# Another order for the five engines' queues in a graph-attention and expert-attention kernel

## The chip, the cores and the metric

The kernel runs on one core of one Trainium2 chip. The metric is device time in microseconds of one execution, taken as the median of several. The profile is that of one execution on the same core.

## The reference

Two layers on `x` of shape 128 graphs x 128 tokens x 384 channels, `adj` of 128 x 128 x 128:

```python
# layer A: graph attention, 12 heads of 32
h = layernorm(x)
q, k = h @ Wq.T, h @ Wk.T;  v = h @ Wv.T + bv
scores = einsum('bqhd,bkhd->bhqk', q, k) * 384**-0.5 + 2 * adj
p = softmax(scores)                  # rows without any score that is not 0 are left out
x = x + einsum('bhqk,bkhd->bqhd', p, v).reshape(b, n, 384) @ Wo.T + bo
# layer B: three causal attention experts of 128 channels, gated
h = layernorm(x)
gate = softmax(relu(h @ Wg1 + bg1) @ Wg2 + bg2)   # the two largest, renormalised: w_e
for e in range(3):
    qe, ke = parts of h @ Wqk + bqk; ve = h @ Wv[e] + bv[e]
    if e == 0: qe = depthwise_conv3(qe)           # e == 1: 4 more keys, all of them masked
    y[e] = softmax(causal(qe @ ke.T / sqrt(128))) @ ve
x = x + (y * w_e).reshape(...) @ Wp + bp
```

## The kernel before, in words

The 128 graphs are worked in 32 groups of 4 (`GB`). The work on a group is cut into steps. A step is named stage.kind.part (`A` for the first layer, `B` for the second, `W` for the weights' preparation at the start), and each engine has its own list of the steps in which it has a share. TensorE (PE) makes the product, ScalarE (ACT) and VectorE (DVE) take it out of its PSUM bank, GpSimd (POOL) scales, and SyncE (SP) issues transfers. The kinds:

- `hT`: four transposes of the normalised input. ACT writes the high f16 part, DVE the low part (what is left), and both feed later products. `qk.0` to `qk.5`: the projections to q and k, nine matmuls each (three passes over split operands). For A, ACT writes the high half and DVE the low one. `v.b`: the value projection of graph b.
- `A.score.b.c`: four heads of graph b (c = 0, 1, 2). DVE adds the adjacency and takes the row minimum into the single buffer `raw_score`, ACT exponentiates into `S[b % 2]`. `smax.b` is one DVE reduction over all of `raw_score`, and `norm.b` makes row factors on DVE and has POOL scale `S` with them. `B.score.b` is the same for three experts. `turn`: transposes of the scaled scores, copied out by ACT. `mix`: scores times values. `proj`: output projection, with the residual added by DVE. `ln1`, `ln2`: layernorm statistics on DVE, the rest on POOL. `res`: POOL adds a bias row to a whole group (1,536 columns). `B.gate.0/1/2` and `B.conv`: chains of small DVE instructions.
- `A.stack.0` and `A.stack.1` (SP): 12 transfers each, which restack q and k of the next group into `Qs` and `Ks`. `A.score.0.0` of that group waits for both of them. `stack.0` waits for the low half of `qk.2` and for the last score product of the group before, `stack.1` for the low half of `qk.5`. `A.adj` and `A.res` load the next adjacencies and inputs, `B.proj` stores.

Products of A go round 5 PSUM banks (`A_RING`), those of B round 3. A product waits until the step that stands 5 (3) places earlier among those of its stage in PE's list has been taken out (`wait_bank`). Bank, place and wait counts all follow from the lists, so the lists alone set the order of work.

A turn of the steady list `ORDER_OF_STEPS` works on three groups at once: the `hT`, `qk` and `stack` of A run one group ahead (`ahead`), the rest of A is on the group of the turn, and B is one group behind A. `FIRST_STEPS` is a list for the weights and the first two turns. Turns 2 to 33 take the steady list; in turn 32 what would be group 32 is left out, and turn 33 has B of group 31 alone. (Below, turn t begins with the product `A.score.0.0` of group t - 1.)

Of the kernel before, what the change touches and what calls it, by code (L numbers as in the profile page):

```python
# [46 lines left out]
NG = NB // GB  # L47
# [41 lines left out]
        W.turn.0@0 W.spread.0@0  # L89
        A.hT.0@0 A.hT.1@0 A.hT.2@0 A.qk.0@0 A.qk.1@0 A.qk.2@0 A.qk.3@0 W.turn.1@0 A.qk.4@0 W.spread.1@0  # L90
        A.qk.5@0 A.v.0@0 A.v.1@0 A.v.2@0 A.v.3@0 A.hT.0@1 A.hT.1@1 A.hT.2@1
        W.turn.2@0 W.spread.2@0 A.qk.0@1
        A.score.0.0@0 A.score.0.1@0 A.score.0.2@0 A.qk.1@1 A.score.1.0@0 A.qk.2@1
        A.score.1.1@0 A.score.1.2@0 A.qk.3@1 A.turn.0.0@0 A.turn.0.1@0 A.turn.0.2@0 A.score.2.0@0 A.mix.0@0
        A.score.2.1@0 A.score.2.2@0 A.qk.4@1 A.proj.0@0 A.turn.1.0@0 A.turn.1.1@0 A.turn.1.2@0
        A.score.3.0@0 A.mix.1@0 A.score.3.1@0 A.score.3.2@0 A.qk.5@1 A.proj.1@0 A.turn.2.0@0
        A.turn.2.1@0 A.turn.2.2@0 A.mix.2@0 A.proj.2@0 A.turn.3.0@0 A.turn.3.1@0 A.turn.3.2@0 A.mix.3@0 A.proj.3@0
    """,
    "act": """
        W.hi.0@0 A.hT.0@0 A.hT.1@0 A.hT.2@0 W.hi.1@0 A.qk.0@0 A.qk.1@0 A.qk.2@0 A.qk.3@0 A.qk.4@0  # L100
        W.hi.2@0 A.qk.5@0 W.stack.1@0 A.hT.0@1 A.hT.1@1 A.hT.2@1 W.hi.3@0 W.hi.4@0 A.qk.0@1 A.score.0.0@0 A.score.0.1@0
        A.qk.1@1 A.score.0.2@0 A.score.1.0@0 A.qk.2@1 A.score.1.1@0 A.score.1.2@0 A.qk.3@1
        A.turn.0.0@0 A.turn.0.1@0 A.turn.0.2@0 A.score.2.0@0 A.mix.0@0 A.score.2.1@0 A.score.2.2@0 A.qk.4@1
        A.turn.1.0@0 A.turn.1.1@0 A.turn.1.2@0 A.score.3.0@0 A.mix.1@0 A.score.3.1@0 A.score.3.2@0 A.qk.5@1
        W.hi.5@0 W.hi.6@0 A.turn.2.0@0 A.turn.2.1@0 A.turn.2.2@0 A.mix.2@0 A.turn.3.0@0 A.turn.3.1@0
        A.turn.3.2@0 A.mix.3@0 W.hi.7@0
    """,
    "dve": """
        W.max.0@0 W.max.1@0 W.share.0@0 W.scale.0@0 W.max.2@0 W.lo.0@0 A.hT.0@0 A.hT.1@0 A.hT.2@0
        W.lo.1@0 W.unit.0@0 A.qk.0@0 W.max.4@0 A.qk.1@0 W.max.5@0 A.qk.2@0 W.max.7@0 A.qk.3@0  # L110
        W.scale.1@0 A.qk.4@0 W.lo.2@0 A.qk.5@0 W.unit.1@0 W.values.0@0 A.v.0@0 A.v.1@0 A.ln1@0 A.v.2@0 W.max.3@0
        A.v.3@0 W.max.6@0 A.hT.0@1 A.hT.1@1 A.hT.2@1 W.scale.2@0 W.bias.0@0 W.unit.2@0 W.lo.3@0 W.lo.4@0 A.qk.0@1 A.score.0.0@0 A.score.0.1@0
        A.score.0.2@0 A.smax.0@0 A.qk.1@1 A.score.1.0@0 A.norm.0@0 A.qk.2@1 A.score.1.1@0 A.score.1.2@0
        A.smax.1@0 A.qk.3@1 A.norm.1@0 A.score.2.0@0 A.mix.0@0 A.score.2.1@0 A.score.2.2@0 A.smax.2@0
        A.qk.4@1 A.proj.0@0 A.norm.2@0 A.score.3.0@0 A.mix.1@0 A.score.3.1@0 A.score.3.2@0 A.smax.3@0
        A.qk.5@1 W.lo.5@0 A.proj.1@0 A.norm.3@0 W.lo.6@0 A.ln2.0@0 A.ln2.1@0 A.mix.2@0 A.proj.2@0
        A.ln2.2@0 A.mix.3@0 A.proj.3@0 A.ln2.3@0 W.lo.7@0
# [958 lines left out]
```

## Time and profile before

| | |
|---|---|
| median of 3 runs (lowest, highest) | 2308.9 us (2306.32, 2308.97) |
| the profiled execution's own time | 2308.58 us |
| its span from first to last instruction | 2306.8 us |
| PE, DVE, ACT, POOL busy | 2224.1, 1926.3, 1496.3, 1094.7 us |
| granted TensorE clock over the span | 0.99 |

The span is what the trace covers; the time is 1.8 us longer. A busy time is the union of an engine's instructions. An instruction that waits for a port or a semaphore inside its own execution counts as busy, so a duration that is above the usual one for its form is a wait too. In the timeline each row has the start in us from the span's start, the duration in us, the engine, the line, the operation with its tiles, how many instructions were merged, and in brackets how long the engine stood idle before it and what ended that.

### The profile page before, as it was taken

To read this page: it belongs to the slowest core of one execution; us is meant where nothing else is said; L and a number is where in the kernel's file an instruction comes from. 1 tells how busy PE (TensorE), PEld (TensorE's weight loads), DVE (VectorE), ACT (ScalarE), POOL (GpSimd) and SP (SyncE) were. 2 spreads that over 40 slices of the span, in tenths; PEclk is the share of its full clock that TensorE was granted. 3 is DMA by queue.
4 is the path that set the end of the run, shared out by engine and by line. 5 is a ranking of instruction groups with operands and counts; after the bars stand their busy time and mean duration, and the time that the engine had idled before them with its cause. 6 is when DMAs were issued, how large, how long until landed. Compare 5 with 4: busy or idle time off the path is not lost.

```text
span 2306.8 us, 51218 instructions
## 1 busy us (share of the span) xinstructions
PE 2224.1 (96%) x16905; PEld 1435.7 (62%) x16905; DVE 1926.3 (84%) x7160; ACT 1496.3 (65%) x5290; POOL 1094.7 (47%) x1351
## 2 busy tenths in 40 slices
PE   6799999999999999999999999999999999999998
PEld 3466666666666666666666666666666666666665
DVE  7788888888888888888888888888888888888884
ACT  2676666676666676666676666676666766666763
POOL 2454455444454544554544554544554544554442
PEclk9899999999999999999999999999999999999999
DMA  5221122221222221222221222211222211222100
GB/s 171 47 64 46 53 74 74 74 47 42 60 74 74 63 53 43 65 74 74 57 53 41 72 74 74 52 51 47 74 75 74 50 46 53 74 74 74 47 15 28
DMA packets 142263, 143.18 MB, mean 62 GB/s; under 512 B 16816, under 2 KB 141360, under 8 KB 142000
## 3 DMA queue, kind: packets, MB, share of 16 engines
q1 hardware_dynamic: 139808, 138.62, 22.6%
q8 instruction: 137, 2.24, 0.4%
q10 hardware_dynamic: 2192, 1.29, 0.2%
q14 instruction: 126, 1.03, 0.1%
HBM read 39.18 MB, written 25.17 MB: 28 GB/s over the span
## 4 chain that ended last, share of the span: by engine, by line
PE 81%; DVE 13%; issue 4%; ACT 1%; POOL 0%; DMA 0%; DVEq 0%; ACTq 0%; POOLq 0%
PE A_bank L465 29%; PE B_bank L465 28%; PE A_bank L536 7%; PE A_bank L548 4%; PE B_bank L555 4%; PE A_bank L523 4%; DVE raw_score L876 2%; PE B_bank L530 2%; PE B_bank L540 2%; PE B_bank L502 2%; DVE g_tmp L810 1%; DVE V L865 1%; DVE q2raw L798 1%; DVE x L916 1%; DVE g_tmp L801 1%
## 5 line engine op out<-in xcount | busy, mean ns | idle before, releaser
L1003 POOL TENSOR_TENSOR S<-S,rowf 128x512 f32<-128x512 f32 x384 | 389.0, 1041 | 663.2 <-DVE rowf L901 663.2
L638 ACT ACTIVATE S<-raw_score,smin 128x128 f32<-128x128 f32 x1536 | 593.7, 392 | 140.5 <-DVE smin L876 140.4
L876 DVE CUSTOM_DVE_ANT_0 raw_score<-A_bank,adj,s_unit 128x128 f32<-128x128 f32 x1536 | 442.5, 346 | 29.9 <-PE A_bank L523 29.7
L638 ACT ACTIVATION_READ_ACCUMULATOR S<-raw_score,smin 128x1 f32 x1536 | 294.7, 192 | 0.0
L652 ACT ACTIVATE PT<-A_bank 128x512 f32<-128x512 f32 x384 | 216.5, 592 | 106.7 <-PE A_bank L536 106.7
L1008 POOL TENSOR_TENSOR S<-S,row2f 128x384 f32<-128x384 f32 x128 | 105.9, 827 | 323.8 <-DVE row2f L909 321.2
L536 PE MATMUL A_bank<-ident,S 128*128 128x128 f32 x1536 | 218.7, 276 | 31.8 <-DVE x L916 29.6
L882 DVE TENSOR_REDUCE smax<-raw_score 128x12 f32<-128x1536 f32 x128 | 224.4, 1753 | 4.4
L536 PEld LDWEIGHTS A_bank<-ident,S 128*128 128x128 f32 x1536 | 181.3, 142 | 58.0 <-DVE x L916 35.3
L645 ACT ACTIVATE S<-S,s2min 128x128 f32<-128x128 f32 x384 | 148.8, 391 | 39.8 <-DVE s2min L886 39.8
L656 ACT ACTIVATE yT_hi<-B_bank 128x384 f16<-128x384 f32 x128 | 62.1, 485 | 164.1 <-PE B_bank L555 164.1
L523 PE MATMUL A_bank<-Ks,Qs 96*128 96x128 f16 x1536 | 134.4, 220 | 3.5 <-DVE k_lo L854 1.6
L465 PE MATMUL B_bank<-wv2g_hi,b_hT_hi 128*128 128x416 f16 x384 | 130.4, 339 | 0.0
L465 PE MATMUL B_bank<-wv2g_hi,b_hT_lo 128*128 128x416 f16 x384 | 130.1, 339 | 0.0
L465 PE MATMUL B_bank<-wv2g_lo,b_hT_hi 128*128 128x416 f16 x384 | 130.1, 339 | 0.0
L465 PE MATMUL A_bank<-wo_hi,oT_hi 128*128 128x384 f16 x384 | 125.9, 328 | 3.8 <-DVE oT_lo L859 3.8
L523 PEld LDWEIGHTS A_bank<-Ks,Qs 96*128 96x128 f16 x1536 | 108.2, 98 | 32.6 <-issue 7.3
L921 DVE SCALAR_TENSOR_TENSOR x1res<-B_bank,p_unit,x1res 128x384 f32<-128x384 f32 x128 | 78.8, 615 | 59.4 <-PE B_bank L465 59.4
L465 PE MATMUL A_bank<-wv_hi,a_hT_hi 128*128 128x384 f16 x384 | 125.4, 327 | 1.9 <-issue 1.5
L876 DVE DVE_READ_ACCUMULATOR2_ANT smin<- 128x1 f32 x1536 | 126.3, 82 | 0.0
L465 PE MATMUL A_bank<-wo_lo,oT_hi 128*128 128x384 f16 x384 | 126.0, 328 | 0.0
L465 PE MATMUL A_bank<-wo_hi,oT_lo 128*128 128x384 f16 x384 | 125.9, 328 | 0.0
(182 smaller groups left out, 6201.0 us busy)
## 6 DMA issues: line engine op xcount, KB each, us to landing
xin<-in_x SPq DMA_DIRECT2D x32, 768.0 KB, 4.7
Qs<-q_hi SPq DMA_DIRECT2D x256, 96.0 KB, 2.2
out<-x1res SPq DMA_DIRECT2D x128, 192.0 KB, 1.9
Ks<-k_hi SPq DMA_DIRECT2D x252, 96.0 KB, 2.6
Qs<-q_lo SPq DMA_DIRECT2D x128, 96.0 KB, 2.2
Ks<-k_lo SPq DMA_DIRECT2D x126, 96.0 KB, 2.2
adj<-in_adj SPq DMA_DIRECT2D x32, 256.0 KB, 3.5
S<-in_wq SPq DMA_DIRECT2D x1, 576.0 KB, 5.6
```

The lines of the kernel that those rows point to most:

```text
L465: mm = nc.tensor.matmul(dst, left(c)[a], right(c)[b], start=(c == 0 and n == 0), stop=(c == KC - 1 and n == 2))
L523: mm = nc.tensor.matmul(dst[:, tok(j)], Qs[:, c * HPC + j, tok(b)], Ks[:, c * HPC + j, tok(b)], start=True, stop=True)
L536: mm = nc.tensor.transpose(dst[:, tok(j)], S[b % 2][:, c * HPC + j, :], ident[:])
L548: mm = nc.tensor.matmul(dst[j * HD:(j + 1) * HD, tok(k)], V[:, b, h * HD:(h + 1) * HD], PT[k][:, tok(j)], start=True, stop=True)
L555: mm = nc.tensor.matmul(dst[:, tok(e)], V2[:, b, e * P:(e + 1) * P], PT2[b % 2][:, tok(e)], start=True, stop=True)
L638: ins = nc.scalar.activation(S[b % 2][:, h, :], raw_score[:, h, :], ACT.Exp, bias=smin[b % 2][:, h:h + 1], scale=-1.0, accum_out=ssum[b % ...
L645: ins = nc.scalar.activation(S2[b % 2][:, e, :], S2[b % 2][:, e, :], ACT.Exp, bias=s2min[b % 2][:, e:e + 1], scale=-1.0, accum_out=s2sum[b ...
L652: nc.scalar.activation(dst, src[:, 0:dst.shape[1]], ACT.Copy).then_inc(evacuated[stage, "act"], 1)
L876: ins = nc.vector.tensor_tensor_reduce(raw_score[:, h, :], src[:, j * T:(j + 1) * T], adj2[:, b, :], s_unit[:], 3.0e38, ALU.add, ALU.min, ...
L882: nc.vector.tensor_reduce(smax[b % 2][:], raw_score[:], AXX, ALU.max).then_inc(maxed, 1)
L1003: nc.gpsimd.tensor_tensor(S[b % 2][:, hs, :], S[b % 2][:, hs, :], rowf[b % 2][:, hs].unsqueeze(2).broadcast_to([P, HPC, T]), ALU.mult).the ...
L1008: nc.gpsimd.tensor_tensor(S2[b % 2][:], S2[b % 2][:], row2f[b % 2][:].unsqueeze(2).broadcast_to([P, NE, T]), ALU.mult).then_inc(normed2, 1)
```

## The change

No step's own instructions change, and every list has the same steps for the same groups as before. Changed are:

- the order in `FIRST_STEPS` (weights and the first two turns): among others `A.hT@1` and `A.qk@1` of PE move from before the first scores to between them, and `W.turn.2`, `W.spread.2` from behind `A.hT@1` to ahead of `A.v.0@0`
- the order in `ORDER_OF_STEPS` for PE, ACT, DVE and POOL (SP's is the same)
- turns 32 and 33, which no longer take the steady list but a new one, `LAST_STEPS`, in which the steps of groups 30 and 31 stand mixed (`@1` is group 30, `@0` is group 31)
- two waits on DVE that the new order needs (`w_lo`), both in the first two groups only

```diff
--- before.py
+++ after.py
@@ -86,79 +86,123 @@
 
 FIRST_STEPS = {
     "pe": """
...
+        W.turn.0@0 W.spread.0@0 A.hT.0@0 A.hT.1@0 A.hT.2@0 A.qk.0@0 A.qk.1@0 A.qk.2@0 A.qk.3@0 W.turn.1@0
+        W.spread.1@0 A.qk.4@0 A.qk.5@0 W.turn.2@0 W.spread.2@0 A.v.0@0 A.v.1@0 A.score.0.0@0 A.score.0.1@0
+        A.score.0.2@0 A.v.2@0 A.score.1.0@0 A.score.1.1@0 A.v.3@0 A.hT.0@1 A.hT.1@1 A.score.1.2@0 A.turn.0.0@0
+        A.turn.0.1@0 A.hT.2@1 A.score.2.0@0 A.score.2.1@0 A.qk.0@1 A.turn.0.2@0 A.qk.1@1 A.mix.0@0 A.score.2.2@0
+        A.turn.1.0@0 A.turn.1.1@0 A.qk.2@1 A.score.3.0@0 A.turn.1.2@0 A.score.3.1@0 A.qk.3@1 A.score.3.2@0
+        A.qk.4@1 A.mix.1@0 A.proj.0@0 A.turn.2.0@0 A.qk.5@1 A.turn.2.1@0 A.turn.2.2@0 A.proj.1@0 A.mix.2@0
+        A.turn.3.0@0 A.turn.3.1@0 A.turn.3.2@0 A.mix.3@0 A.proj.2@0 A.proj.3@0
     """,
     "act": """
...
     """,
     "dve": """
...
+        W.max.0@0 W.max.1@0 W.share.0@0 W.scale.0@0 W.unit.0@0 A.hT.0@0 W.lo.0@0 W.max.2@0 A.hT.1@0 A.hT.2@0
+        W.max.4@0 W.lo.1@0 A.qk.0@0 A.qk.1@0 W.max.7@0 A.qk.2@0 W.max.5@0 A.qk.3@0 W.max.3@0 W.scale.1@0
+        A.qk.4@0 W.max.6@0 A.qk.5@0 W.unit.1@0 W.lo.2@0 W.values.0@0 A.ln1@0 W.scale.2@0 A.v.0@0 A.v.1@0
+        A.score.0.0@0 A.score.0.1@0 A.v.2@0 A.score.0.2@0 A.smax.0@0 A.hT.0@1 A.score.1.0@0 A.norm.0@0 A.v.3@0
+        A.score.1.1@0 A.score.1.2@0 A.hT.1@1 A.smax.1@0 A.hT.2@1 A.score.2.0@0 W.unit.2@0 A.norm.1@0
+        A.score.2.1@0 A.qk.0@1 W.lo.3@0 A.qk.1@1 A.score.2.2@0 A.mix.0@0 A.smax.2@0 A.qk.2@1 A.score.3.0@0
+        A.score.3.1@0 A.score.3.2@0 A.qk.3@1 A.norm.2@0 W.lo.4@0 A.qk.4@1 A.proj.0@0 A.smax.3@0 A.mix.1@0
+        A.norm.3@0 A.qk.5@1 W.lo.5@0 A.proj.1@0 W.lo.6@0 A.ln2.0@0 A.mix.2@0 W.lo.7@0 A.ln2.1@0 A.proj.2@0
+        A.mix.3@0 A.ln2.2@0 W.bias.0@0 A.proj.3@0 A.ln2.3@0
     """,
     "pool": """
-        A.res@0 A.ln1@0 A.norm.0@0 A.norm.1@0 A.norm.2@0 A.ln2.0@0 A.norm.3@0 A.adj@0 A.ln2.1@0 A.ln2.2@0 A.ln2.3@0
+        A.res@0 A.ln1@0 A.norm.0@0 A.norm.1@0 A.norm.2@0 A.norm.3@0 A.adj@0 A.ln2.0@0 A.ln2.1@0 A.ln2.2@0
+        A.ln2.3@0
     """,
     "sp": """
-        A.res@0 A.stack.0@0 A.stack.1@0 A.adj@0 A.stack.0@1 A.stack.1@1
+        A.res@0 A.stack.0@0 A.stack.1@0 A.stack.0@1 A.adj@0 A.stack.1@1
     """,
 }
 
 ORDER_OF_STEPS = {
     "pe": """
-        A.score.0.0 A.v.0 A.score.0.1 A.v.1 A.score.0.2 A.v.2 A.v.3 B.hT.0 B.hT.1 A.score.1.0 B.hT.2
-        A.score.1.1 A.score.1.2 B.qk.0 B.qk.1 B.qk.2 B.v.0 A.turn.0.0 A.turn.0.1 B.qk.3 B.v.1
-        A.turn.0.2 A.score.2.0 B.v.2 A.mix.0 A.score.2.1 A.score.2.2 B.v.3 B.qk.4 B.qk.5 A.proj.0
-        B.score.0 A.hT.0 A.hT.1 A.turn.1.0 A.hT.2 B.score.1 A.turn.1.1 A.qk.0 A.turn.1.2 A.score.3.0
-        A.score.3.1 A.qk.1 A.qk.2 A.score.3.2 B.turn.0 A.qk.3 A.mix.1 A.qk.4 B.score.2 A.qk.5
-        A.turn.2.0 A.turn.2.1 B.turn.1 A.turn.2.2 A.proj.1 B.score.3 A.mix.2 B.mix.0 A.turn.3.0
-        A.turn.3.1 B.mix.1 A.turn.3.2 A.proj.2 B.turn.2 A.mix.3 B.proj.0 A.proj.3 B.mix.2 B.turn.3
-        B.proj.1 B.mix.3 B.proj.2 B.proj.3
+        A.score.0.0 A.score.0.1 A.v.0 A.v.1 A.score.0.2 B.hT.0 B.hT.1 B.hT.2 A.score.1.0 A.score.1.1 A.v.2
+        B.qk.0 B.v.0 B.v.1 A.score.1.2 B.qk.1 B.v.2 A.turn.0.0 A.v.3 A.turn.0.1 B.v.3 B.qk.2 A.turn.0.2 B.qk.3
+        A.hT.0 A.score.2.0 A.hT.1 A.mix.0 A.score.2.1 B.qk.4 A.hT.2 B.qk.5 A.turn.1.0 A.proj.0 B.score.0
+        A.turn.1.1 B.score.1 A.score.2.2 A.qk.0 A.turn.1.2 A.score.3.0 A.qk.1 A.qk.2 A.qk.3 B.turn.0 A.qk.4
+        B.mix.0 A.score.3.1 A.mix.1 A.score.3.2 B.turn.1 B.score.2 A.turn.2.0 A.qk.5 A.turn.2.1 A.proj.1
+        A.turn.2.2 B.score.3 B.mix.1 B.proj.0 A.mix.2 B.turn.2 B.proj.1 A.turn.3.0 B.mix.2 A.turn.3.1 A.turn.3.2
+        A.proj.2 B.turn.3 A.mix.3 B.mix.3 B.proj.2 A.proj.3 B.proj.3
     """,
     "act": """
...
+        A.score.0.0 B.hT.0 B.hT.1 B.hT.2 A.score.0.1 A.score.0.2 B.qk.0 A.turn.0.0 B.qk.1 A.score.1.0 A.turn.0.1
+        A.score.1.1 A.turn.0.2 B.qk.2 A.hT.0 A.score.1.2 A.hT.1 B.gate.0 A.mix.0 B.qk.3 A.hT.2 B.qk.4 B.qk.5
+        A.turn.1.0 A.score.2.0 A.turn.1.1 A.score.2.1 A.qk.0 B.gate.1 B.score.0 A.qk.1 A.turn.1.2 A.score.2.2
+        B.score.1 A.qk.2 B.turn.0 A.qk.3 A.qk.4 A.score.3.0 B.mix.0 A.mix.1 B.turn.1 A.turn.2.0 A.score.3.1
+        B.score.2 A.score.3.2 A.turn.2.1 A.turn.2.2 B.mix.1 A.qk.5 A.mix.2 B.turn.2 B.score.3 A.turn.3.0 B.mix.2
+        A.turn.3.1 A.turn.3.2 B.turn.3 A.mix.3 B.mix.3
     """,
     "dve": """
-        A.score.0.0 A.score.0.1 A.v.0 A.score.0.2 A.smax.0 A.v.1 B.hT.0 B.hT.1 B.hT.2 A.score.1.0
-        A.norm.0 A.ln1 A.v.2 A.v.3 A.score.1.1 B.conv B.v.0 A.score.1.2 A.smax.1 A.score.2.0 B.v.1 B.v.2
-        A.score.2.1 B.v.3 A.mix.0 B.gate.0 A.norm.1 B.gate.1 A.score.2.2 A.smax.2 A.proj.0 A.hT.0 A.hT.1
-        A.hT.2 B.score.0 B.gate.2 B.norm.0 B.score.1 A.qk.0 A.score.3.0 A.score.3.1 B.norm.1 A.qk.1
-        A.qk.2 A.norm.2 A.score.3.2 A.smax.3 A.ln2.0 A.mix.1 A.qk.3 B.score.2 A.qk.4 A.qk.5 A.norm.3
-        B.norm.2 B.score.3 A.proj.1 B.mix.0 A.mix.2 A.ln2.1 B.norm.3 A.proj.2 A.mix.3 A.ln2.2 B.mix.1
-        B.proj.0 A.proj.3 A.ln2.3 B.mix.2 B.proj.1 B.mix.3 B.proj.2 B.proj.3
+        A.score.0.0 A.v.0 A.score.0.1 A.score.0.2 B.hT.0 B.hT.1 B.hT.2 A.smax.0 A.v.1 A.score.1.0 B.v.0 A.norm.0
+        A.score.1.1 A.ln1 A.v.2 B.v.1 A.score.1.2 B.v.2 A.v.3 B.conv B.v.3 A.smax.1 B.gate.0 A.hT.0 A.norm.1
+        A.hT.1 A.score.2.0 A.mix.0 A.hT.2 A.score.2.1 B.gate.1 B.score.0 A.proj.0 A.score.2.2 B.score.1 B.gate.2
+        A.qk.0 B.norm.0 A.smax.2 A.qk.1 A.score.3.0 B.norm.1 A.norm.2 A.qk.2 A.qk.3 A.qk.4 A.score.3.1 A.mix.1
+        B.score.2 A.score.3.2 B.mix.0 A.smax.3 B.norm.2 A.norm.3 B.score.3 B.mix.1 A.qk.5 A.proj.1 B.proj.0
+        A.mix.2 B.norm.3 A.ln2.0 B.proj.1 A.ln2.1 B.mix.2 A.proj.2 A.mix.3 A.ln2.2 B.mix.3 B.proj.2 A.proj.3
+        A.ln2.3 B.proj.3
     """,
     "pool": """
-        A.res A.norm.0 A.ln1 B.res A.norm.1 B.norm.0 B.norm.1 A.norm.2 A.ln2.0 A.norm.3 A.adj
-        B.norm.2 A.ln2.1 B.norm.3 A.ln2.2 A.ln2.3
+        A.res A.norm.0 A.ln1 B.res A.norm.1 B.norm.0 B.norm.1 A.norm.2 B.norm.2 A.norm.3 B.norm.3 A.ln2.0
+        A.ln2.1 A.adj A.ln2.2 A.ln2.3
     """,
     "sp": """
         A.res A.stack.0 A.adj A.stack.1 B.proj.0 B.proj.1 B.proj.2 B.proj.3
+    """,
+}
+
+LAST_STEPS = {
+    "pe": """
+        A.score.0.0@0 A.score.0.1@0 A.v.0@0 A.score.0.2@0 B.hT.0@1 A.v.1@0 B.hT.1@1 A.score.1.0@0 B.hT.2@1
+        B.qk.0@1 B.v.0@1 A.score.1.1@0 A.score.1.2@0 B.v.1@1 B.v.2@1 B.qk.1@1 B.v.3@1 A.turn.0.0@0 A.score.2.0@0
+        B.qk.2@1 B.qk.3@1 B.qk.4@1 A.turn.0.1@0 A.score.2.1@0 A.turn.0.2@0 B.qk.5@1 A.score.2.2@0 B.score.0@1
+        A.mix.0@0 A.turn.1.0@0 A.turn.1.1@0 B.score.1@1 A.turn.1.2@0 A.score.3.0@0 A.v.2@0 A.score.3.1@0
+        B.turn.0@1 A.score.3.2@0 B.score.2@1 A.mix.1@0 A.proj.0@0 A.turn.2.0@0 A.turn.2.1@0 B.mix.0@1 B.turn.1@1
+        A.proj.1@0 A.turn.2.2@0 A.v.3@0 A.mix.2@0 A.turn.3.0@0 A.turn.3.1@0 A.turn.3.2@0 B.mix.1@1 B.proj.0@1
+        A.mix.3@0 A.proj.2@0 A.proj.3@0 B.score.3@1 B.turn.2@1 B.proj.1@1 B.mix.2@1 B.hT.0@0 B.hT.1@0 B.proj.2@1
+        B.hT.2@0 B.turn.3@1 B.qk.0@0 B.qk.1@0 B.mix.3@1 B.v.0@0 B.v.1@0 B.v.2@0 B.v.3@0 B.qk.2@0 B.qk.3@0
+        B.qk.4@0 B.qk.5@0 B.score.0@0 B.score.1@0 B.proj.3@1 B.turn.0@0 B.score.2@0 B.turn.1@0 B.mix.0@0
+        B.score.3@0 B.mix.1@0 B.proj.0@0 B.turn.2@0 B.mix.2@0 B.turn.3@0 B.proj.1@0 B.mix.3@0 B.proj.2@0
+        B.proj.3@0
+    """,
+    "act": """
...
+    """,
+    "dve": """
...
+    """,
+    "pool": """
+        A.norm.0@0 A.norm.1@0 B.res@1 A.res@0 B.norm.0@1 A.norm.2@0 B.norm.1@1 A.norm.3@0 A.ln2.0@0 A.ln2.1@0
+        B.norm.2@1 A.ln2.2@0 A.ln2.3@0 B.norm.3@1 A.adj@0 B.norm.0@0 B.norm.1@0 B.res@0 B.norm.2@0 B.norm.3@0
+        A.ln1@0
+    """,
+    "sp": """
+        A.adj@0 B.proj.0@1 A.res@0 B.proj.1@1 B.proj.2@1 B.proj.3@1 B.proj.0@0 B.proj.1@0 B.proj.2@0 B.proj.3@0
     """,
 }
 
@@ -180,12 +224,13 @@
     first = [parse(word) for word in FIRST_STEPS.get(engine, "").split()]
     order = [parse(word) for word in ORDER_OF_STEPS[engine].split()]
     program = list(first)
-    for turn in range(2 if first else 0, NG + 2):
+    last = [parse(word) for word in LAST_STEPS.get(engine, "").split()]
+    for turn in range(2 if first else 0, NG if last else NG + 2):
         for step in order:
             group = turn - (0 if ahead(step) else 1 if step[0] == "A" else 2)
             if 0 <= group < NG:
                 program.append((step, group))
-    return program
+    return program + [(step, NG - 1 - back) for step, back in last]
 
 
 GATE_LINKS = 17
@@ -861,6 +906,8 @@
                                             ALU.subtract).then_inc(freed, 1)
                 elif kind == "v":
                     wait_products(dve, step, g)
+                    if g == 0 and not A:
+                        dve.wait_ge(w_lo, len(raw))
                     V_b, row, col = (V[:, b, :], bv_row, 0) if A else (V2[:, b, :], bvg_row, 1)
                     nc.vector.scalar_tensor_tensor(out=V_b, in0=src[:, 0:row.shape[1]], scalar=v_unit[:, col:col + 1],
                                                    in1=row[:], op0=ALU.mult, op1=ALU.add).then_inc(freed, 1)
@@ -911,7 +958,9 @@
                     wait_products(dve, step, g)
 
                     dve.wait_ge(xres_ready, count(g, 1, 1))
-                    if not g == 0:
+                    if g == 0:
+                        dve.wait_ge(w_lo, 5)
+                    else:
                         dve.wait_ge(x1res_ready, count(g, 1, 0))
                     nc.vector.scalar_tensor_tensor(out=x1[:, b, :], in0=src[:, 0:C], scalar=p_unit[:, 0:1],
                                                    in1=xres[:, b, :], op0=ALU.mult, op1=ALU.add).then_inc(freed, 1)
```

## Rows read from the trace of the kernel before

**Rows 1.** The page: span, engine totals, the chain that ended last.

```profile
span 2306.8 us, 51218 instructions
PE 2224.1 (96%) x16905; PEld 1435.7 (62%) x16905; DVE 1926.3 (84%) x7160; ACT 1496.3 (65%) x5290; POOL 1094.7 (47%) x1351
PE 81%; DVE 13%; issue 4%; ACT 1%; POOL 0%; DMA 0%; DVEq 0%; ACTq 0%; POOLq 0%
```

**Rows 2.** Windows by stage: start:end, length, busy time of each engine, clock, DMA.

```profile
core 0: us, PE busy (x) PEld busy (x) DVE busy (x) ACT busy (x) POOL busy (x), PEclk, DMA share, GB/s
...
53.30:105.90 52.60, 36.16 (x275) 21.70 (x274) 35.64 (x138) 33.58 (x121) 17.84 (x25) 0.80 0.22 51
...
664.50:734.20 69.70, 68.68 (x531) 44.45 (x529) 59.19 (x222) 46.35 (x165) 34.20 (x43) 1.00 0.23 62
...
2198.00:2262.50 64.50, 59.91 (x464) 40.72 (x462) 54.98 (x205) 42.01 (x156) 26.96 (x34) 0.92 0.04 14
2262.50:2306.80 44.30, 35.76 (x200) 22.84 (x198) 19.75 (x70) 15.43 (x44) 6.74 (x5) 0.92 0.08 28
...
105.90:2198.00 2092.10, 2060.78 (x15841) 1333.70 (x15840) 1777.44 (x6663) 1390.93 (x4950) 1030.59 (x1265) 1.00 0.23 61
```

**Rows 3.** Timeline of turn 10 on PE: `B.score.1`, `turn.1.1`, `qk.0`; `B.score.2`.

```profile
697.95 0.83 PE L530 MATMUL B_bank<-k,q 128*128 128x128 f32 x6
699.77 0.66 PE L536 MATMUL A_bank<-ident,S 128*128 128x128 f32 x4 [0.99 <-DVE x L916]
700.46 0.38 PE L465 MATMUL A_bank<-a_hT_hi,wq_hi 128*128 128x512 f16 x1
...
712.51 0.83 PE L530 MATMUL B_bank<-k,q 128*128 128x128 f32 x6
713.18 0.38 PE L465 MATMUL A_bank<-a_hT_hi,wk_hi 128*128 128x512 f16 x1
```

**Rows 4.** The same turn, DVE: `smax.2` and `A.proj.0`; all waits for A products.

```profile
697.43 1.75 DVE L882 TENSOR_REDUCE smax<-raw_score 128x12 f32<-128x1536 f32 x1
699.10 0.61 DVE L916 SCALAR_TENSOR_TENSOR x<-A_bank,p_unit,xres 128x384 f32<-128x384 f32 x1
...
PE A_bank L536 <- DVE x L916: 29.6, 30, 1.0
```

**Rows 5.** K restack in turn 10: `qk.5` low half, SP's issues; landing medians.

```profile
715.95 0.69 DVE L854 SCALAR_TENSOR_TENSOR k_lo<-A_bank,k_hi 128x512 f16<-128x512 f32 x1 [0.60 <-ACT k_hi L613]
...
717.68 3.78 SPq L440 DMA_DIRECT2D Ks<-k_hi  x4
...
724.08 2.56 SPq L440 DMA_DIRECT2D Ks<-k_hi  x4
...
Ks<-k_hi SPq DMA_DIRECT2D x8, 96.0 KB, 2.4
```

**Rows 6.** DVE instructions with two SBUF operands, against POOL (turns 10 and 32).

```profile
694.42 0.82 DVE L810 TENSOR_TENSOR g_tmp<-g_tmp,g_col 128x12 f32<-128x12 f32 x1
694.17 3.05 POOL L1003 TENSOR_TENSOR S<-S,rowf 128x512 f32<-128x512 f32 x3 [6.91 <-DVE rowf L901]
...
2213.08 3.81 DVE L938 SCALAR_TENSOR_TENSOR q<-q2raw,conv_neg,q 128x508 f32<-128x508 f32 x1
2212.46 3.89 POOL L997 TENSOR_TENSOR x1res<-x,bp_row 128x1536 f32<-128x1536 f32 x1
```

**Rows 7.** Opening: PE ahead of `hT@1`, DVE and POOL steps, the last K issues.

```profile
32.48 0.68 DVE L854 SCALAR_TENSOR_TENSOR k_lo<-A_bank,k_hi 128x512 f16<-128x512 f32 x1
...
53.27 1.15 PE L523 MATMUL A_bank<-Ks,Qs 96*128 96x128 f16 x11
...
97.34 3.04 POOL L1003 TENSOR_TENSOR S<-S,rowf 128x512 f32<-128x512 f32 x3
...
89.56 0.69 DVE L854 SCALAR_TENSOR_TENSOR k_lo<-A_bank,k_hi 128x512 f16<-128x512 f32 x1 [0.86 <-ACT k_hi L613]
...
101.17 2.54 SPq L440 DMA_DIRECT2D Ks<-k_hi  x4
```

More of the change, by code:

```diff
@@ L88 @@
     "pe": """
[L89 to L95, printed above, removed]
@@ L96 @@
-        A.score.3.0@0 A.mix.1@0 A.score.3.1@0 A.score.3.2@0 A.qk.5@1 A.proj.1@0 A.turn.2.0@0
-        A.turn.2.1@0 A.turn.2.2@0 A.mix.2@0 A.proj.2@0 A.turn.3.0@0 A.turn.3.1@0 A.turn.3.2@0 A.mix.3@0 A.proj.3@0
+        W.turn.0@0 W.spread.0@0 A.hT.0@0 A.hT.1@0 A.hT.2@0 A.qk.0@0 A.qk.1@0 A.qk.2@0 A.qk.3@0 W.turn.1@0
+        W.spread.1@0 A.qk.4@0 A.qk.5@0 W.turn.2@0 W.spread.2@0 A.v.0@0 A.v.1@0 A.score.0.0@0 A.score.0.1@0
+        A.score.0.2@0 A.v.2@0 A.score.1.0@0 A.score.1.1@0 A.v.3@0 A.hT.0@1 A.hT.1@1 A.score.1.2@0 A.turn.0.0@0
@@ L98 @@
+        A.turn.0.1@0 A.hT.2@1 A.score.2.0@0 A.score.2.1@0 A.qk.0@1 A.turn.0.2@0 A.qk.1@1 A.mix.0@0 A.score.2.2@0
+        A.turn.1.0@0 A.turn.1.1@0 A.qk.2@1 A.score.3.0@0 A.turn.1.2@0 A.score.3.1@0 A.qk.3@1 A.score.3.2@0
+        A.qk.4@1 A.mix.1@0 A.proj.0@0 A.turn.2.0@0 A.qk.5@1 A.turn.2.1@0 A.turn.2.2@0 A.proj.1@0 A.mix.2@0
+        A.turn.3.0@0 A.turn.3.1@0 A.turn.3.2@0 A.mix.3@0 A.proj.2@0 A.proj.3@0
     """,
     "act": """
-        W.hi.0@0 A.hT.0@0 A.hT.1@0 A.hT.2@0 W.hi.1@0 A.qk.0@0 A.qk.1@0 A.qk.2@0 A.qk.3@0 A.qk.4@0
@@ L101 @@
[L101 to L105, printed above, removed]
@@ L106 @@
-        A.turn.3.2@0 A.mix.3@0 W.hi.7@0
+        A.hT.0@0 W.hi.0@0 W.hi.1@0 A.hT.1@0 A.hT.2@0 A.qk.0@0 A.qk.1@0 A.qk.2@0 A.qk.3@0 A.qk.4@0 A.qk.5@0
+        W.hi.2@0 W.stack.1@0 W.hi.3@0 W.hi.4@0 A.score.0.0@0 A.score.0.1@0 A.hT.0@1 A.score.0.2@0 A.hT.1@1
+        A.score.1.0@0 A.score.1.1@0 A.turn.0.0@0 A.hT.2@1 A.turn.0.1@0 W.hi.5@0 A.score.1.2@0 A.qk.0@1
+        A.turn.0.2@0 A.score.2.0@0 A.qk.1@1 A.mix.0@0 W.hi.6@0 A.turn.1.0@0 A.turn.1.1@0 A.score.2.1@0 A.qk.2@1
+        A.score.2.2@0 A.turn.1.2@0 A.qk.3@1 A.score.3.0@0 W.hi.7@0 A.qk.4@1 A.score.3.1@0 A.mix.1@0
@@ L107 @@
+        A.score.3.2@0 A.turn.2.0@0 A.qk.5@1 A.turn.2.1@0 A.turn.2.2@0 A.turn.3.0@0 A.mix.2@0 A.turn.3.1@0
+        A.turn.3.2@0 A.mix.3@0
     """,
     "dve": """
[L109 to L117, printed above, removed]
+        W.max.0@0 W.max.1@0 W.share.0@0 W.scale.0@0 W.unit.0@0 A.hT.0@0 W.lo.0@0 W.max.2@0 A.hT.1@0 A.hT.2@0
@@ L137 @@
+        A.turn.1.1 B.score.1 A.score.2.2 A.qk.0 A.turn.1.2 A.score.3.0 A.qk.1 A.qk.2 A.qk.3 B.turn.0 A.qk.4
+        B.mix.0 A.score.3.1 A.mix.1 A.score.3.2 B.turn.1 B.score.2 A.turn.2.0 A.qk.5 A.turn.2.1 A.proj.1
+        A.turn.2.2 B.score.3 B.mix.1 B.proj.0 A.mix.2 B.turn.2 B.proj.1 A.turn.3.0 B.mix.2 A.turn.3.1 A.turn.3.2
+        A.proj.2 B.turn.3 A.mix.3 B.mix.3 B.proj.2 A.proj.3 B.proj.3
     """,
     "act": """
-        A.score.0.0 A.score.0.1 B.hT.0 B.hT.1 B.hT.2 A.score.0.2 B.qk.0 A.score.1.0 B.qk.1 B.qk.2
@@ L140 @@
-        A.turn.0.0 A.turn.0.1 B.qk.3 A.score.1.1 A.turn.0.2 A.score.1.2 A.mix.0 A.score.2.0
-        A.score.2.1 B.gate.0 B.qk.4 B.qk.5 A.hT.0 A.hT.1 A.turn.1.0 B.gate.1 A.hT.2 A.turn.1.1
-        B.score.0 A.qk.0 A.score.2.2 A.turn.1.2 B.score.1 A.qk.1 A.qk.2 A.score.3.0 A.score.3.1
-        A.mix.1 A.qk.3 A.qk.4 B.turn.0 A.score.3.2 A.qk.5 B.score.2 A.turn.2.0 B.turn.1 A.turn.2.1
-        A.turn.2.2 A.mix.2 B.mix.0 A.turn.3.0 A.turn.3.1 A.turn.3.2 B.score.3 B.mix.1 B.turn.2
-        A.mix.3 B.mix.2 B.turn.3 B.mix.3
+        A.score.0.0 B.hT.0 B.hT.1 B.hT.2 A.score.0.1 A.score.0.2 B.qk.0 A.turn.0.0 B.qk.1 A.score.1.0 A.turn.0.1
```

19 lines of the change are left out of this document (added).

## The prediction, made before the changed kernel was run

> **What bounds the kernel now.** I read the page first. PE is busy for 96% of the span and holds 81% of the chain that ended last; DVE has 84% and 13% [rows 1]. A busy share is a mean over stages, so I next cut the span where `A.score.0.0` of a group starts [rows 2]. Thirty steady turns take 105.9 to 2198.0, 2092.1 us, so 69.74 us each. What lies around them is 105.9 us ahead and 108.8 us behind (64.5 and 44.3). In a steady turn the clock is full and PE is busy for 68.68 of 69.70 us; ACT with 46 us and POOL with 34 us have much room, DVE with 59 us has some. In turn 1 PE is busy for 36.2 of 52.6 us at a mean clock of 0.80, in the last window for 35.8 of 44.3 us. So a new order can win little per turn, but thirty times, and it can win more per microsecond at the two ends.
>
> The timeline of PE in a steady turn shows where the idle microsecond lies. `B.score.1` starts at 697.95, and the next product, `A.turn.1.1`, starts 1.82 us later; after `B.score.2` the same distance is 0.67 us [rows 3]. That is a stall of 1.15 us. The four transposes of `turn.1.1` then take 0.69 us up to `qk.0`; four in a row elsewhere take 0.44 us, which is 0.25 us more. What ends the wait is DVE's `A.proj.0`: five places back in A's ring of banks stands `proj.0`, and DVE takes it out at 699.10 only, since `smax.2` (1.75 us) stands ahead of it in DVE's list [rows 4]. The view of waits has this 30 times, 29.6 us, once a turn [rows 4]. It costs 1.15 + 0.25 = 1.40 us a turn.
>
> **The change, part by part.** *The steady turn.* Nothing is added or removed, so PE's work in a turn stays, and the best turn is 69.74 - 1.40 = 68.34 us. (Small delays of about 0.05 to 0.1 us at four other places, together 0.26 us, may go or stay. I leave them in the sum; 68.1 us is the low bound.) In the new list the product five places ahead of `turn.1.1` is `mix.0`, not `proj.0`. To see when DVE is done with it I laid the new lists side by side, gave each step the duration that it has in turn 10, started PE at 0 with no stall, and let each step of ACT, DVE and POOL begin when its list and its input allow. DVE takes `mix.0` out at 29.4 us, and PE wants the bank at 32.9: 3.5 us to spare. The same walk gives the other tight places: `A.proj.0` needs `mix.0` 1.3 us before its turn; `A.turn.1.0` needs the bank of `score.2.0` with 1.4 us to spare; `A.turn.3.0` waits for the low half of `qk.5` with 2 us to spare; `B.mix.3` gets its transposes from ACT with 0.2 us to spare, which is thin, but a miss there costs tenths. `B.hT.0` wants all of `ln2` from POOL 1.6 us after it is ready. No place costs a whole microsecond, and I find no new stall.
>
> *What gets later: the K restack.* Before, DVE takes `qk.5` at 715.95 and is done at about 716.6. SP issues 12 transfers from 717.68 to 726.64 and the last lands 2.4 us later, near 729.0 [rows 5], 5.2 us before the next turn. In the new lists `qk.5` starts on PE 48.2 us after the turn's start (48.7 before), but on ACT and DVE it stands behind `B.mix.1`, whose product ends 4 us later still. The walk has its low half done at 56.0 us. From SP's first Ks issue to the last landing is 11.4 us by the rows, so Ks is there at 67.5 us, and the next `A.score.0.0` wants it at 68.3. Of 5.2 us of cover 0.8 is left. `A.adj`, queued on SP between the two stacks, is issued before `qk.5` is done and adds nothing; `B.proj`'s stores are behind and wait at most 1 us, which nobody waits for before `B.res` of the next turn. This is the thinnest cover of the change. The cost is 0 if the walk is right, and x - 0.8 us a turn if `qk.5` is x late. The nearest row for x is an `L938` of 3.81 us, 3.06 us over its usual 0.75 [rows 6]; the lower end is 0. I take 0, since DVE has several waits ahead of `qk.5` that absorb a delay.
>
> *Ports.* DVE instructions that read two SBUF operands stretch while POOL runs: `L810`, 12 columns, takes 0.82 us and ends with POOL's first 1.04 us piece of `norm.1`, and the second `B.conv` instruction of turn 32 takes 3.81 us beside POOL's `B.res` [rows 6]. In the new turn `gate.1` falls behind `norm.1` (about 1.3 us of DVE saved) and the multiplications of `gate.0` start about 1 us before `B.res` is through (1 us lost); `conv` still meets `ln1`. That nets out near nothing. Were `B.conv` laid under `B.res` every turn, that would be rival 2. The rule for such pairs stands in the Trainium skill, page "SBUF — State Buffer", section "SBUF: two separate sides": GpSimd and VectorE share a port pair as an exclusive lock, held for a whole instruction. The trace agrees with it in both pairs of rows; by that rule the change would come out at rival 2's time instead of mine if the two meet.
>
> So 30 turns at 68.34 give 2050.2 instead of 2092.1: **-42 us**. Bounds: 68.1 us gives -49; 69.2 (half of the gain lost in new small waits) gives -16.
>
> *The opening.* `A.score.0.0@0` starts at 53.27 now [rows 7], behind `hT@1` and `qk.0@1`. In the new list only two of the `v` steps, `W.turn.2` and `W.spread.2` stand ahead. `W.spread.2` waits for a DVE reduction, which in DVE's list follows `qk.5@0` (done at 33.1 now [rows 7], about 2 us later in the new list because `W.scale.1` moves ahead of `qk.4` on PE), `W.unit.1`, `W.lo.2`, `W.values` and `ln1@1`. These have 0.5 + 1.3 + 2.9 + 2.3 = 7.0 us, so it comes at 42.5. PE is idle for some 8 us there, its clock falls to half, and `v.0` and `v.1` take 2.9 us each, twice their length in a steady turn: first scores at 49, 4 us earlier. Next, DVE does `smax.3` and `norm.3@0` ahead of the splits `W.lo.5` to `W.lo.7`, where before `lo.5` and `proj.1` stood ahead of `norm.3`, and POOL did `ln2.0` ahead of it. POOL starts `norm.3` at 97.34 now [rows 7], at about 86 in my walk. The low half of `qk.5@1` is done at 90.2 now, and the last K issue ends at 103.7, the last landing just before turn 2 starts at 105.9 [rows 7]. The walk has `qk.5@1` at 86, and 11.4 us later Ks is there: 97.4. Turn 2 starts at 98: **-8 us**. Bounds: 0 if the half clock and the small steps eat it; -12 if the chain follows the first K at once.
>
> *The close.* PE is busy for 59.9 + 35.8 = 95.7 of 108.8 us [rows 2], some of it at half clock. Now `B.hT.0@31` comes at 64.5 us after the start of turn 32 and 44.3 us are left. In `LAST_STEPS` it has 51 us of PE's work ahead, and four steps of group 30 (`B.proj.2`, `turn.3`, `mix.3`, `proj.3`, 3.9 us) are kept for the gaps of group 31. The walk meets about 6 us of waits on the way (`v.2` for `mix.0`'s bank 2.6, `B.turn.0` 1.2, `B.qk.0` 1.3, `ln2.3` 1.0) and reaches `B.hT.0@31` at 57.5. The rest takes 44.3 + 3.9 - 2.4 (gaps filled) = 45.8 us. Together 103.3: **-5 us**. Bounds: -1 and -9.
>
> The sum: 2308.6 (the profiled execution's own time) - 42 - 8 - 5 = 2253.6; the median of the runs is 0.3 us above that execution, so **2254 us**.
>
> **Rivals.** *1, the K restack arrives late.* For it: 4.4 of its 5.2 us of cover go, and my walk has an error of a microsecond or so over 56 us. Against it: DVE's waits ahead absorb. One microsecond late beyond the cover makes a turn 69.34: -12 - 13 = 2283 us. It decides the sign when `qk.5`'s low half is more than 0.8 + 1.40 + 13/30 = 2.6 us later than I have it; at 4 us late a turn is 71.5 us, +54 - 13 = 2349 us, **slower**. This is the rival on the other side.
> *2, the port.* `B.conv`'s second instruction stands behind `B.res` every turn (3.06 us). For it: turn 32 shows it, and POOL starts `B.res` as soon as `ln1` is through, 1.5 us after `conv` begins. Against it: both hang on DVE's `ln1`, so their distance is fixed, and `conv` is 1.0 us early enough; DVE has two waits of 0.8 and 0.9 us behind it. Then 1.4 us are left at `score.2.0`, and they would cost PE up to 1 us: turn 69.3, 2282 us.
> *3, only the steady turn changes.* The ends give nothing since PE's half clock comes back in each new gap: 2308.9 - 42 = 2267 us.
> *4, nothing changes.* Another bank wait of the same size takes the place of the old, and the ends are even: 2309 us.
>
> **How the numbers follow.** My forecast (turn of 68.1 to 68.7 us, both ends shorter) has a chance of 0.64; rival 3 has 0.12; rivals 1 (below its deciding point) and 2 together 0.12; rival 4 0.03; rival 1 beyond its point 0.09. 0.2% is 4.6 us and is about what a measurement can tell from no change. Faster by more than that: 0.64 + 0.12 + 0.12 = 0.88; within: 0.04 (rival 4 and the edge of rival 1); slower: 0.08. The forecast's own range is 2308.9 - 49 - 12 - 9 = 2239 to 2308.9 - 32 - 3 - 1 = 2273. To hold 8 in 10 it goes up to rivals 1 and 2, 2286, and a little below the low sum: 2236 to 2286.
>
> **What would show it.** Right: the wait of `L536` for DVE's `x` (30 times) is gone, PE's start of `A.score.0.0` repeats each 68.1 to 68.7 us, Ks's last landing is 0 to 2 us before it, turn 2 starts at 98 +- 4, and 101 to 107 us lie behind the start of turn 32. Wrong: PE waits in `L523` once a turn for the restack (rival 1); `L938` or `L798` above 3 us once a turn (rival 2); turn 2 still past 103 (rival 3); a different wait of about a microsecond 30 times (rival 4).

## The result and the profile after

The changed kernel takes 2256.3 us, median of 4 runs (2256.0 to 2256.4), against 2308.9 (2306.3 to 2309.0) for the kernel before on the same chip. The ratio is 0.9775 [0.9758, 0.9791]: faster, by 2.2%. Predicted was 2254 us.

The page of after, parts 1 and 4 (its profiled execution took 2256.1 us). Where lines of this kernel are named, they stand 45 to 49 further down than in the kernel before: `L465` is `L510`, `L523` is `L568`, `L530` is `L575`, `L536` is `L581`, `L854` is `L899`.

```profile
span 2254.3 us, 51222 instructions
PE 2200.9 (98%) x16905; PEld 1435.5 (64%) x16905; DVE 1916.8 (85%) x7160; ACT 1495.3 (66%) x5290; POOL 1115.9 (49%) x1351
PE 94%; DVE 4%; issue 1%; POOL 1%; ACT 1%; DMA 0%; SPq 0%; DVEq 0%; ACTq 0%; POOLq 0%
```

Against [rows 1] the chain that ended last has moved to PE, 94% instead of 81%, and DVE holds 4% instead of 13%. The windows of after, cut at the same events as [rows 2]: turn 1, turn 10, the two parts of the close, all 30 steady turns.

```profile
core 0: us, PE busy (x) PEld busy (x) DVE busy (x) ACT busy (x) POOL busy (x), PEclk, DMA share, GB/s
50.10:96.60 46.50, 37.06 (x313) 23.29 (x312) 43.45 (x154) 34.72 (x124) 21.84 (x22) 0.96 0.25 58
642.40:710.60 68.20, 68.20 (x531) 44.68 (x530) 58.84 (x223) 46.37 (x165) 34.78 (x42) 1.00 0.24 63
2142.20:2207.60 65.40, 54.03 (x437) 36.18 (x435) 56.54 (x202) 40.55 (x153) 29.80 (x37) 0.95 0.03 10
2207.60:2254.30 46.70, 38.55 (x225) 23.54 (x225) 21.81 (x74) 16.76 (x48) 7.56 (x6) 0.96 0.07 26
96.60:2142.20 2045.60, 2045.44 (x15841) 1340.19 (x15842) 1762.56 (x6662) 1390.83 (x4950) 1044.48 (x1264) 1.00 0.24 63
```

What the reader is to see: in the steady turns PE is busy for 2045.44 of 2045.60 us, so its own work, in this order, sets the turn. Before it was busy for 2060.78 of 2092.10 us [rows 2]: of the 46.5 us won there, 31.2 were idle time and 15.3 busy time. The two windows of the close are longer than before, 112.1 us against 108.8.

| Stage | before | after | difference | predicted |
|---|---|---|---|---|
| to the start of turn 2 | 105.9 | 96.6 | -9.3 | -8 |
| 30 steady turns | 2092.1 | 2045.6 | -46.5 | -42 |
| from the start of turn 32 | 108.8 | 112.1 | **+3.3** | **-5** |
| sum | 2306.8 | 2254.3 | -52.5 | -55 |

Waits on PE, the whole run of after: us in total, times, the longest.

```profile
PE B_bank L523 <- DVE wmax L730: 12.1, 3, 10.6
PE B_bank L527 <- DVE top_col L744: 10.1, 3, 7.6
PE B_bank L575 <- ACT k L675: 7.7, 2, 6.8
...
PE A_bank L581 <- DVE smin L923: 1.8, 1, 1.8
...
PE A_bank L568 <- DMA Ks<-k_hi: 0.2, 1, 0.2
```

The wait of [rows 4], 30 times at `turn.1.1`, has gone, and no other wait comes more than 3 times. Most of what is left is at the two ends: `L523` and `L527` are the reductions over the weights, and `L575` with 6.8 us is new, in the close.

**The close.** DVE and POOL of after behind the start of turn 32, where `B.gate.0` of group 30 runs, and the product on PE that waits for it.

```profile
2164.61 3.13 POOL L1052 TENSOR_TENSOR S<-S,rowf 128x512 f32<-128x512 f32 x3 [5.41 <-DVE rowf L948]
2164.70 3.19 DVE L843 TENSOR_TENSOR q2raw<-g_hid,wg_row 128x128 f32<-128x128 f32 x3
2167.70 3.47 POOL L1046 TENSOR_TENSOR x1res<-x,bp_row 128x1536 f32<-128x1536 f32 x1
2167.92 0.55 DVE L846 TENSOR_REDUCE g_tmp<-q2raw 128x12 f32<-128x384 f32 x1
2168.51 2.69 DVE L847 TENSOR_TENSOR g_tmp<-g_tmp,bg_row 128x12 f32<-128x12 f32 x1
2171.14 3.41 POOL L1036 TENSOR_TENSOR xres<-xin,bo_row 128x1536 f32<-128x1536 f32 x1
2171.24 0.17 DVE L848 TENSOR_REDUCE g_col<-g_tmp 128x4 f32<-128x12 f32 x1
2171.44 3.14 DVE L850 TENSOR_TENSOR g_tmp<-g_tmp,g_col 128x12 f32<-128x12 f32 x1
...
2176.93 1.40 PE L575 MATMUL B_bank<-k,q 128*128 128x128 f32 x5 [6.81 <-ACT k L675]
```

Three instructions of `B.gate.0` read two SBUF operands (`L843`, `L847`, `L850`). Each ends within 0.2 us of one of three POOL steps that stand in a row in `LAST_STEPS`: `norm.1` (3.13), `B.res` (3.47), `A.res` (3.41). On 12 columns, where the two take 0.17 us elsewhere (`e6` below), `L847` takes 2.69 and `L850` 3.14. The step takes 10.1 us. ACT's half of `gate.0` waits for it, `qk.3` to `qk.5` are queued behind that on ACT, and `B.score.0` on PE waits 6.81 us for `k`. The granted clock falls during that wait: it is 0.50 from 2173.4 to 2180.2 (3.27 of 6.80 us busy).

**The K restack.** DVE and SP of after in turn 10, which starts at 642.35; turn 11 starts at 710.53.

```profile
697.77 0.69 DVE L899 SCALAR_TENSOR_TENSOR k_lo<-A_bank,k_hi 128x512 f16<-128x512 f32 x1
...
699.15 2.51 SPq L485 DMA_DIRECT2D Ks<-k_hi  x4
701.70 2.54 SPq L485 DMA_DIRECT2D Ks<-k_lo  x4
704.28 2.55 SPq L485 DMA_DIRECT2D Ks<-k_hi  x4
```

`qk.5`'s low half is done 56.1 us after the turn's start. The first Ks issue starts 0.7 us behind that. The three fours of issues take 7.7 us here; in [rows 5] they take 9.0, since one issue among them takes 1.87 us instead of 0.60. Over the turns the twelve take 7.7 to 9.2 us in either kernel, with medians of 8.4 before and 8.3 after. The last transfer lands 2.2 us behind the start of its issue, at 66.1 us of the turn, 2.1 us before it is wanted (median over the turns 1.9, from 0.65 to 2.5). By the same landing times the cover was 5.9 us in turn 10 of before, and 6.4 in the median.

### The profile page after: what moved, and what is told of

Read it like the earlier page. It is cut to its first block, busy times and chain, and to the rows that moved or that the text cites. A ratio compares the mean times of both kernels' runs of the same rounds, so it can differ in the third digit from the quotient of the medians.

```text
span 2254.3 us, 51222 instructions
## 1 busy us (share of the span) xinstructions
PE 2200.9 (98%) x16905; PEld 1435.5 (64%) x16905; DVE 1916.8 (85%) x7160; ACT 1495.3 (66%) x5290; POOL 1115.9 (49%) x1351
## 4 chain that ended last, share of the span: by engine, by line
PE 94%; DVE 4%; issue 1%; POOL 1%; ACT 1%; DMA 0%; SPq 0%; DVEq 0%; ACTq 0%; POOLq 0%
PE B_bank L510 33%; PE A_bank L510 32%; PE A_bank L581 7%; PE A_bank L593 4%; PE B_bank L600 4%; PE A_bank L568 4%; PE B_bank L575 4%; PE B_bank L585 2%; PE B_bank L547 2%; PE A_bank L547 2%; DVE raw_score L923 1%; DVE smax L929 0%; DVE wmax L730 0%; DMA S<-in_wk 0%; POOL h L1070 0%
## 5 line engine op out<-in xcount | busy, mean ns | idle before, releaser
L581 PE MATMUL A_bank<-ident,S 128*128 128x128 f32 x1536 | 225.5, 274 | 3.3 <-DVE smin L923 1.8
L581 PEld LDWEIGHTS A_bank<-ident,S 128*128 128x128 f32 x1536 | 186.8, 141 | 40.1 <-DVE smin L923 2.0
L568 PE MATMUL A_bank<-Ks,Qs 96*128 96x128 f16 x1536 | 139.3, 220 | 2.6 <-DVE smin L923 2.4
L510 PE MATMUL B_bank<-wv2g_hi,b_hT_hi 128*128 128x416 f16 x384 | 130.2, 339 | 0.0
L510 PE MATMUL B_bank<-wv2g_hi,b_hT_lo 128*128 128x416 f16 x384 | 130.2, 339 | 0.0
L510 PE MATMUL B_bank<-wv2g_lo,b_hT_hi 128*128 128x416 f16 x384 | 130.2, 339 | 0.0
L568 PEld LDWEIGHTS A_bank<-Ks,Qs 96*128 96x128 f16 x1536 | 108.4, 98 | 31.2 <-issue 7.1
L510 PE MATMUL B_bank<-wp_hi,yT_hi 128*128 128x384 f16 x384 | 125.6, 327 | 2.1 <-DVE yT_lo L904 2.1
L510 PE MATMUL A_bank<-wo_hi,oT_hi 128*128 128x384 f16 x384 | 125.2, 326 | 2.1 <-DVE oT_lo L904 2.1
L510 PE MATMUL A_bank<-wv_hi,a_hT_hi 128*128 128x384 f16 x384 | 126.5, 329 | 0.7 <-DVE oT_lo L904 0.4
L510 PE MATMUL A_bank<-wv_hi,a_hT_lo 128*128 128x384 f16 x384 | 126.3, 329 | 0.0
L510 PE MATMUL A_bank<-wv_lo,a_hT_hi 128*128 128x384 f16 x384 | 126.3, 329 | 0.0
L510 PE MATMUL B_bank<-wp_hi,yT_lo 128*128 128x384 f16 x384 | 125.6, 327 | 0.0
```

Source lines behind the costliest of these rows:

```text
L510: mm = nc.tensor.matmul(dst, left(c)[a], right(c)[b], start=(c == 0 and n == 0), stop=(c == KC - 1 and n == 2))
L568: mm = nc.tensor.matmul(dst[:, tok(j)], Qs[:, c * HPC + j, tok(b)], Ks[:, c * HPC + j, tok(b)], start=True, stop=True)
L581: mm = nc.tensor.transpose(dst[:, tok(j)], S[b % 2][:, c * HPC + j, :], ident[:])
```

## The experiments

The kernel before was timed beside each, with medians of 2307.6 to 2308.5 us. Where an edit is to the changed kernel, the ratio is still to the kernel before. The experiments ran on other chips than the run of after, and the kernel before itself differs by 1.3 us between them. The intervals of `e5` to `e8` overlap that of after, so for differences of 3 to 6 us the stages of the profiled executions have to speak too. These vary as well, by 1 to 2 us at each end from one execution to another.

| Run | median us | ratio to before |
|---|---|---|
| after | 2256.3 | 0.9775 [0.9758, 0.9791] |
| e1_proj0_first (of before) | 2304.0 | 0.9984 [0.9975, 0.9993] |
| e10_smax2_behind_hT (of before) | 2304.1 | 0.9981 [0.9972, 0.9990] |
| e2_steady_only | 2269.2 | 0.9832 [0.9818, 0.9845] |
| e3_first_only | 2296.5 | 0.9952 [0.9940, 0.9965] |
| e4_last_only | 2312.2 | 1.0019 [1.0011, 1.0028] |
| e5_ares_early (of after) | 2252.2 | 0.9759 [0.9745, 0.9772] |
| e6_both_res_early (of after) | 2249.7 | 0.9749 [0.9736, 0.9763] |
| e7_scale2_early (of after) | 2253.6 | 0.9764 [0.9751, 0.9778] |
| e8_one_store_first (of after) | 2259.5 | 0.9791 [0.9778, 0.9805] |
| e9_two_stores_first (of after) | 2367.7 | 1.0248 [1.0232, 1.0265] |
| e11_res_and_scale2 | 2245.4 | 0.9727 [0.9714, 0.9741] |
| e12_gate_first | 2244.9 | 0.9727 [0.9714, 0.9741] |

**The parts alone.** `e2` has the new steady lists, which also close (`LAST_STEPS` is left out), and the old opening; `e3` has the new opening alone; `e4` has `LAST_STEPS` alone.

> The new steady list with the old opening, and turns 32 and 33 by the steady list too. Theory: turns of 68.2 us, 30 x 1.57 = 47 us less in turns 2 to 31, the ends within a few us of before: 2258 to 2264 us. Rival (the ends carry part of it): above 2266 us.

> The new opening alone, with the old steady list and the old close. Theory: turn 2 starts at 96 to 98 instead of 105.9, and nothing is given back: 2298 to 2301 us. Rival (the steady turn absorbs an early start, since its period is set by another loop): 2305 us or more.

> The new list for turns 32 and 33 alone, with the old opening and the old steady list. Theory (gate.0 of group 30 stands under POOL's norm.1, B.res and A.res for 10 us and delays B.score.0 by 7 us): the close is 3 us longer than before, 2311 to 2313 us. Rival (the close is longer only because it follows the new steady list): 2303 to 2307 us.

In `e2` every turn but the first is 68.17 us (2046.5 for the 30), and the whole is 38.5 us under before, less than its theory had. The close is 114.5 us: the new steady lists close 5.7 us worse than the old ones. In `e3` turn 2 starts at 95.7 and a turn is 69.67: -11.2 us, a little more than its theory had. `e4` is 4.5 us slower than before, [1.0011, 1.0028], as expected, with the same 6.8 us of wait at `B.score.0`, a `gate.0` of 10.12 us and a close 4.9 us longer than before's. So `LAST_STEPS` loses 3 to 5 us against the old close, and wins 2.3 against the one it replaces (112.1 against 114.5). The three medians sum to -38.5 - 11.2 + 4.5 = -45.2; `after` has -52.6. By the profiled stages most of the 7.4 us between them is the close: `e2` and `e4` each have a longer one, 10.6 us together, where `after` has 3.3. The steady turns and the opening nearly add up: the turns are 45.7 us shorter in `e2` and 46.5 in `after`, the start of turn 2 is 10.1 us earlier in `e3` and 9.3 in `after`.

**Was it `smax.2` ahead of `A.proj.0`?** Two edits of the kernel before, to DVE's steady list; the second also moves `smax.2` behind `hT`.

```
e1:   A.score.2.2 A.smax.2 A.proj.0 A.hT.0 A.hT.1 A.hT.2 B.score.0
   -> A.score.2.2 A.proj.0 A.smax.2 A.hT.0 A.hT.1 A.hT.2 B.score.0
e10: A.score.2.2 A.proj.0 A.hT.0 A.hT.1 A.hT.2 A.smax.2 B.score.0
```

> The kernel before with one swap in DVE's steady list: A.proj.0 ahead of A.smax.2. Theory (the 1.40 us stall of a steady turn is only the bank of turn.1.1, freed late because smax.2 stands ahead): a turn falls from 69.7 to about 68.3 us and the time by some 35 to 42 us, to 2267 to 2274 us, so that the rest of the steady list's new order brings next to nothing. Rival (the old order has other stalls hidden behind this one): less than 20 us, 2289 us or more.

> The kernel before with A.smax.2 moved in DVE's steady list behind A.proj.0 and the three A.hT steps (the swap with A.proj.0 alone had moved PE's stall from turn.1.1 to qk.0, which waits for the low half of hT). Theory (DVE is behind as a whole there, and what it owes PE first are proj.0 and the three low halves): no wait is left at either place, a turn takes 68.2 to 68.5 us, and the time falls by 35 to 45 us, to 2263 to 2273 us. Rival (a third consumer behind smax.2 takes the stall over again, since all of DVE's list is late): a turn stays above 69.2 us and the time above 2293 us.

Waits on PE in `e1`, and the same place of turn 10 on its timeline:

```profile
PE A_bank L465 <- DVE a_hT_lo L848: 34.9, 31, 1.4
...
699.82 0.38 PE L465 MATMUL A_bank<-a_hT_hi,wq_hi 128*128 128x512 f16 x1 [1.12 <-DVE a_hT_lo L848]
```

and in `e10`:

```profile
PE A_bank L465 <- DVE q_lo L854: 34.7, 31, 1.6
...
703.93 0.39 PE L465 MATMUL A_bank<-a_hT_hi,wq_hi 128*128 128x512 f16 x1 [1.09 <-DVE q_lo L854]
```

The wait at `turn.1.1` went both times, and each time one of the same size stood a few products later: at `qk.0` for the split of `hT`, then at `qk.2` for a bank that holds `q`. A turn is 69.55 and 69.53 us, against 69.68 before. Each edit wins 4 us (0.2%) of the 35 to 45 that its theory gave it, so in both the rival held. What the trace shows instead is a stretch of DVE without slack. Waits on DVE of before from 690.7 to 714.9, 24 us of turn 10:

```profile
DVE V L865 <- PE B_bank L465: 0.6, 1, 0.6
DVE r2inv L906 <- ACT S L645: 0.3, 1, 0.3
```

DVE is behind there, and whatever PE wants from it comes late; the view of waits names only the product that meets it first. In turn 10 of after, from `gate.0` on and for 24 us too (664.7 to 689.0), DVE waits four times, 2.6 us in all instead of 0.9:

```profile
DVE S L933 <- PE B_bank L575: 1.1, 1, 1.1
DVE g_tmp L864 <- ACT g_tmp L706: 0.7, 1, 0.7
DVE r2inv L953 <- ACT S L690: 0.5, 1, 0.5
DVE k_lo L899 <- ACT k_hi L658: 0.3, 1, 0.3
```

That speaks for DVE keeping up in the new lists, and is an argument from the trace, not an experiment. It is not a strong one: from 653.7 to 674.3, over 20 us, DVE has no wait at all in after either, and PE does not wait for it there. What `e2` shows is that the new steady lists as a whole take the stall away; which of the moves does it (`hT` and its split earlier, `score.3` later, `smax.2` behind `qk.0`) I did not separate.

**The close.** All three are edits of POOL's list for the last turns, the third with a swap in DVE's.

```
after: A.norm.0@0 A.norm.1@0 B.res@1 A.res@0
e5:    A.res@0 A.norm.0@0 A.norm.1@0 B.res@1
e6:    A.res@0 B.res@1 A.norm.0@0 A.norm.1@0
e12:   as e6 and e7, and on DVE: A.norm.1@0 B.gate.0@1 -> B.gate.0@1 A.norm.1@0
```

> The changed kernel with A.res of group 31 moved to the head of POOL's closing list, where POOL is idle; B.res of group 30 stays behind norm.1. Theory (DVE's gate.0 is shut out by each of POOL's long two-operand instructions in turn): gate.0 of group 30 falls from 10.06 us by one such instruction, 3.4 us, to about 6.6, and the time by about 3.4 us, to 2253 us. Rival (gate.0 waits for something else, such as ACT or its own data): gate.0 stays at 10 us and the time at 2256 us.

> The changed kernel with A.res and B.res both at the head of POOL's closing list, ahead of norm.0. Theory: gate.0 of group 30 is left with norm.1 alone, 3 to 4.5 us, the 6.8 us wait of B.score.0 is gone, and the close is 5 us or more shorter than in the kernel before instead of 3.3 us longer: 2248 to 2250 us. Rival: as for the run with A.res alone, 2256 us.

`e5`, DVE's `L847` and `L850`: one of the two has its normal length again.

```profile
2167.03 2.69 DVE L847 TENSOR_TENSOR g_tmp<-g_tmp,bg_row 128x12 f32<-128x12 f32 x1
2169.96 0.17 DVE L850 TENSOR_TENSOR g_tmp<-g_tmp,g_col 128x12 f32<-128x12 f32 x1
```

`e6`, the same two and what is left, `L843` under `norm.1`:

```profile
2163.91 3.13 POOL L1052 TENSOR_TENSOR S<-S,rowf 128x512 f32<-128x512 f32 x3 [5.41 <-DVE rowf L948]
2164.00 3.19 DVE L843 TENSOR_TENSOR q2raw<-g_hid,wg_row 128x128 f32<-128x128 f32 x3
2167.81 0.17 DVE L847 TENSOR_TENSOR g_tmp<-g_tmp,bg_row 128x12 f32<-128x12 f32 x1
2168.22 0.17 DVE L850 TENSOR_TENSOR g_tmp<-g_tmp,g_col 128x12 f32<-128x12 f32 x1
```

`gate.0` takes 10.1, 7.1 and 4.6 us in `after`, `e5` and `e6`: the two POOL instructions moved away give DVE 3.0 and 2.5 us back. The medians fall by 4.1 and 6.5 us. With `e6` the wait of `B.score.0` is 1.3 us. The profiled closes are 108.0 us in `e5` and 107.8 in `e6`, against 112.1 to 114.1 in the five runs with the unchanged `LAST_STEPS` (`after`, `e4`, `e7`, `e8`, `e9`). That is only 1 us under before's 108.8, where 5 or more were expected of `e6`.

**The opening.** `e7` moves `W.scale.2` on DVE ahead of `W.values` and `ln1@1`, for which `W.spread.2` on PE, 7.57 us idle, had waited.

> The changed kernel with W.scale.2 moved ahead of W.values and A.ln1 in DVE's opening list, so that PE does not stand 7.6 us in W.spread.2. Theory (the opening's chain runs through that wait): v.0 starts some 5 us earlier, the first scores as soon as the restack of group 0 has landed, near 45 us, and the time falls by 2 to 4 us, to 2252 to 2254 us. Rival (the first scores are followed by waits for h1 of group 1, which ln1 now delivers later, and the gain is given back): 2256 us or more.

```profile
38.93 0.38 PE L527 MATMUL B_bank<-ident,top_col 2*128 2x2 f32 x2 [3.12 <-DVE top_col L744]
44.90 1.33 PE L568 MATMUL A_bank<-Ks,Qs 96*128 96x128 f16 x11 [2.56 <-DMA Ks<-k_hi]
```

The first scores come 5.2 us earlier, at 44.90, now behind a wait for the restack; turn 2 starts 3.9 us earlier (92.7), since turn 1 is 1.3 us longer. The median falls by 2.7 us. Of the 3.9 us the profiled execution gives 1.9 back in the close, where no step was moved: 114.1 us, with 6.8 us at the half clock near its end instead of 3.4.

**The cover of the restack.** `e8` puts one store of `B.proj` ahead of `A.stack.1` in SP's steady list, `e9` two.

> The changed kernel with B.proj.0's store ahead of A.stack.1 in SP's steady list. SP then starts the K restack about 0.9 us later. Theory (the last K transfer lands at 66.1 us of a turn and is wanted at 68.2, 2.1 us of cover): within the cover, 2256 us, no change. Rival (no cover: the restack sets the turn's length): 30 x 0.9 = 27 us slower.

> The changed kernel with the stores of B.proj.0 and B.proj.1 ahead of A.stack.1 in SP's steady list, so that the K restack starts when DVE is done with B.proj.1, about 60.4 us into the turn instead of 56.8. Theory (2.1 us of cover in the trace): the last K transfer lands some 3.7 us later, 1.6 us after PE wants it, a turn takes about 69.8 us, and the time rises by some 48 us to 2304 us. Rival (the restack has another 2 us of cover that the trace does not show): below 2270 us.

`e8` loses 3.3 us where its theory had none: the first Ks issue is 0.9 us later, the median cover is 0.5 us, and 5 of the turns are 0.1 to 0.8 us longer. `e9` is 111 us slower than after, more than twice the 48 us expected. Its waits on PE, two of its turns, and the first 3 us of the longer one:

```profile
PE A_bank L568 <- DMA Ks<-k_hi: 71.4, 31, 3.3
...
524.50:597.30 72.80, 69.88 (x528) 45.29 (x529) 58.83 (x222) 46.38 (x165) 34.41 (x43) 0.98 0.22 59
597.30:667.60 70.30, 68.33 (x528) 44.61 (x529) 58.62 (x222) 46.37 (x165) 33.82 (x42) 1.00 0.24 61
...
524.50:527.70 3.20, 3.20 (x16) 1.93 (x17) 1.17 (x8) 1.33 (x7) 2.11 (x1) 0.50 0.14 53
```

PE waits 1.9 to 3.3 us for the restack at each `score.0.0`, 2.3 in the mean. A turn is 71.6 us in the mean, 3.4 more than in after. In the longer turn PE is also busy for 1.7 us more (69.88 against 68.20), since behind the wait the granted clock is 0.50 for a short while; in the shorter one it stays at 1.00, and PE is busy for 0.1 us more. The clock falls so around the start of 16 of the 30 turns. PE is busy for 2075.78 us in the 30 turns, 30.3 more than in after, and the rest of the 101 us by which they are longer is its wait. So the wait is two thirds of the loss, and nearly all of the rest stands in the turns whose start ran at the half clock.

**Together.** `e11` joins `e6` and `e7`; `e12` adds the swap on DVE.

> The changed kernel with A.res and B.res at the head of POOL's closing list and W.scale.2 ahead of W.values and A.ln1 in DVE's opening list. Theory (the two ends are independent): the gains add, 2256.3 - 6.5 - 2.7 = 2247 us. Rival (the clock's state at the ends makes the gains noise): 2249 to 2252 us.

> The run before this one, with B.gate.0 of group 30 ahead of A.norm.1 in DVE's closing list, so that the gate's two-operand multiplications run while POOL is idle. Theory (gate.0's 4.6 us there are still 2.4 us of lock under norm.1): gate.0 takes 2.2 us, B.score.0's wait of 1.3 us goes, and the time falls by 1 to 2 us, to 2245 to 2246 us. Rival (norm.1 is then late for turn.1.0 and PE gives it back): no change against that run.

Against after `e11` wins 10.9 us, a little more than 6.5 + 2.7; by the profiled stages it is 5.0 us in the opening (turn 2 starts at 91.6) and 4.2 in the close (107.9 us). In `e12` all three instructions of `gate.0` have their normal length:

```profile
2159.88 0.70 DVE L843 TENSOR_TENSOR q2raw<-g_hid,wg_row 128x128 f32<-128x128 f32 x3
2161.19 0.17 DVE L847 TENSOR_TENSOR g_tmp<-g_tmp,bg_row 128x12 f32<-128x12 f32 x1
2161.60 0.17 DVE L850 TENSOR_TENSOR g_tmp<-g_tmp,g_col 128x12 f32<-128x12 f32 x1
```

Yet its median is only 0.5 us below `e11`, with runs from 2243.9 to 2248.8, which is no measurable difference. Both are 2.7% faster than before and some 11 us faster than the change.

## Why the prediction came out so

*The stages.* 2254 was said, 2256.3 measured. Of the three terms of the sum two were right and one had the wrong sign. That the total came so close is in part luck: the turns and the opening gave 5.8 us more than said, and the close gave 8.3 us less.

*The steady turn, -42 said, -46.5 measured.* The turn is 68.17 us, near the low bound of 68.1. It was 69.68 in most turns of before, so 1.51 us went and not 1.40: some of the small delays that I left in the sum (0.26 us) went as well. The mean of 69.74 also holds one longer turn, turn 2, which went from 70.91 to 68.53. The statement "No place costs a whole microsecond, and I find no new stall" held: PE is idle for 0.16 us in all 30 turns. The reason given for the old stall was too narrow. That `smax.2` stands ahead of `A.proj.0` is where it showed; removed by itself, it came back twice at the same size (`e1`, `e10`), as the mechanism of rival 4 has it. The forecast survived since the walk laid out all of the new lists and not that one swap. (The bound of 69.2, said to be half of the gain lost, is more than half: 0.86 of 1.40 us.)

*The restack, "Of 5.2 us of cover 0.8 is left".* `qk.5` was placed to 0.1 us (56.0 said, 56.1 measured). The cover is 1.9 us in the median, and was 6.4 us before: I had both too low. The profile counts a landing from the start of an issue, and I counted the 2.4 us from the end of the last one, 0.6 us too late. I also took the 9.0 us of [rows 5] for the usual length of the twelve issues, where the median is 8.3 or 8.4. Against these stands the 0.6 to 0.7 us between `qk.5`'s low half and the first Ks issue, which the walk left out. The rival was real: `e8` shows that after 0.9 us more the cover begins to fail, and `e9`, whose first Ks issue comes 4 us later than in after even in its shorter turns, is slower than before (1.0248). The rival's price of 1 us for each microsecond late fits these shorter turns (70.3 us); it leaves out the half clock behind the wait, which brings the mean turn to 71.6 us.

*Ports in the steady turn, "That nets out near nothing".* They cost PE nothing. `gate.0` takes 3.8 us on DVE in turn 10, of which 1.7 are the time that its first instruction is held beside `B.res` (last section), and not one of the multiplications, as I had it. PE does not wait for it.

*The opening, -8 said, -9.3 measured.* First scores at 50.07 (49 said), PE's idle time at `W.spread.2` 7.57 us (8 said), `norm.3` on POOL at 84.99 (86 said), turn 2 at 96.6 (98 said). `v.0` and `v.1` run at the half clock there, as said: 5.7 us together from 44.34, where `e7`, which reaches them at 39.24 at the full clock, has the same 18 matmuls in 2.9 us.

*The close, -5 said, +3.3 measured.* The step that failed is "The walk meets about 6 us of waits on the way (...) and reaches `B.hT.0@31` at 57.5". It came at 65.4. The 45.8 us said for the rest were 46.7. On the way to `B.hT.0@31` PE is idle for 11.4 us, where about 6 were said, and busy for 54.0, where 51 were said. The walk had no term for the 6.81 us wait: it gave `B.gate.0` of group 30 its usual 2 us. I had looked for pairs of DVE and POOL in the steady turn, where I weighed the Trainium skill's rule on the shared port pair (page "SBUF — State Buffer", section "SBUF: two separate sides"), and not in `LAST_STEPS`, where POOL's list puts `norm.1`, `B.res` and `A.res` in one block of 10 us against that very step. That rule and the rows agree: each of the three DVE instructions ends within 0.2 us of a POOL instruction. In `e12`, with `gate.0` at its normal length, `B.hT.0@31` comes 58.8 us after the start of turn 32, with PE idle for 5.9 us on the way, and the profiled close is 104.3 us: the walk's 57.5 and 103.3 are nearly right for a kernel without the collision. So the collision and what hangs on it account for up to 6.6 of the 7.9 us by which `B.hT.0@31` was later than said. Not all of that is the wait: in this execution, the fastest of four, the clock also stays full through the close, and in `e11`, with `gate.0` at 4.6 us and the clock at 0.97, `B.hT.0@31` comes at 60.7 and the close is 107.9 us.

*The rivals.* Rival 2, the port, was right in its mechanism and wrong in its place: in the close, once, and on `gate.0` instead of `conv`. Rival 3 (only the steady turn gives) was wrong, the opening alone gives 11 us. Rival 4's mechanism is what `e1` and `e10` did.

## What to carry to other kernels

When a wait of the same size comes every turn and names one releaser, look at whether that engine has any wait of its own in the microseconds before. If it has none, it may be behind by a stretch of its list, and then a swap of the two named steps moves the wait instead of removing it, as it did twice here. The swap itself is the test; a stretch without waits is only a hint, since after has one too. When you walk through a new order, walk its short lists as well as the loop: put POOL's long SBUF instructions beside DVE's instructions with two SBUF operands in every list, the last turns too. And when a transfer's cover is cut from 6 to 2 us, shift the transfer by a microsecond or two in an experiment: it shows how near the edge the kernel stands.

## What the runs showed of the hardware

A DVE instruction with one SBUF input was held as well. `L841` writes `g_hid` in SBUF from `V` in SBUF, both f32, and takes 0.22 us in the close. In each of the 30 steady turns of after it starts 1.6 us behind POOL's `B.res`, takes 1.89 us and ends 0.1 us behind it, as here in turn 10:

```profile
663.01 3.44 POOL L1046 TENSOR_TENSOR x1res<-x,bp_row 128x1536 f32<-128x1536 f32 x1
664.65 1.89 DVE L841 TENSOR_SCALAR g_hid<-V 128x128 f32<-128x128 f32 x1
666.57 0.70 DVE L843 TENSOR_TENSOR q2raw<-g_hid,wg_row 128x128 f32<-128x128 f32 x3
```

The profile counts such a hold as busy time: DVE's busy 56.54 us in the first window of the close is 51.18 in `e11`, with the same 202 instructions.

SP starts a transfer of the restack every 0.64 us, so the 12 of them are 7.7 us of the path from `qk.5` to the next turn (up to 9.2 where one takes longer), over three times the 2.2 us from the start of the last one's issue to its landing.

A wait that comes every turn can cost more than itself. In `e9` PE's wait of 1.9 to 3.3 us went with a fall of the granted clock to its half level in 16 of 30 turns, and a mean wait of 2.3 us made the turn 3.4 us longer.
